# VectorE's two-operand work is moved from between a drive and its recurrence to behind the recurrence

## What is computed

```python
x = x + attention(gn(x))      # layer 0: 12 heads of 32, softmax over 1024 keys, a 5x5 depthwise
                              #          term ("lepe"), a gate o, a projection
x = x + selective_scan(gn(x)) # layer 1: 4 directions, 384 channels, 16 states, 1024 steps
x = x + shift_blur(gn(x))     # layer 2: shift by an offset, then a 5x5 Gaussian, per 8 channels
x = x + attention_se(gn(x))   # layer 3: one head, squeeze-and-excite gate, projection, batch norm

def step(h, inp):             # the recurrence of layer 1
    dtt, ut, bt, ct = inp
    dA = jnp.exp(dtt[..., None] * A)
    h = h * dA + (dtt * ut)[..., None] * bt[:, :, None, :]
    y = jnp.einsum('bkdn,bkn->bkd', h, ct)
    return (h, y)
```

## Time and profile before

| what | value |
| --- | --- |
| median of 3 runs | 10391.47 us |
| profiled execution, its own time | 10405.13 us |
| its span in the profile | 10403.3 us |
| VectorE (DVE) busy | 8089.8 us, 78% |
| TensorE (PE) busy | 7344.5 us, 71% |
| GpSimd (POOL) busy | 4789.0 us, 46% |
| ScalarE (ACT) busy | 4060.0 us, 39% |
| mean granted clock of TensorE | 0.786 |

### The profile page before, as it was taken

How to read it: one execution, slowest core, us unless ns; L and a number is a source line. 1 busy time by engine, 2 the same in 40 slices (tenths; PEclk the granted TensorE clock), 3 DMA queues, 4 the chain that set the end, 5 groups by cost and what they waited for, 6 DMA issues and landing times.

```text
span 10403.3 us, 101295 instructions
## 1 busy us (share of the span) xinstructions
PE 7344.5 (71%) x33720; PEld 3729.0 (36%) x33720; DVE 8089.8 (78%) x5527; ACT 4060.0 (39%) x4186; POOL 4789.0 (46%) x1990
## 2 busy tenths in 40 slices
PE   6757775777758777586776777677775777757556
PEld 2233334433334333342234432343333433244333
DVE  5477888778885888768987688876888678887992
ACT  3333443344433444334443345433443334433431
POOL 2154554345553454435644355434555345543660
PEclk8857877888769878688887878787886888868657
DMA  0174457544574445744566445664447544575782
GB/s 26 42 234 160 164 184 235 197 144 165 187 250 164 159 165 201 237 159 160 174 216 220 158 163 170 234 198 162 164 163 246 196 154 160 189 232 198 253 272 58
DMA packets 717961, 1875.97 MB, mean 180 GB/s; under 512 B 258896, under 2 KB 274640, under 8 KB 717264
## 3 DMA queue, kind: packets, MB, share of 16 engines
q1 hardware_dynamic: 717392, 1869.00, 54.0%
HBM read 1772.03 MB, written 71.04 MB: 177 GB/s over the span
## 4 chain that ended last, share of the span: by engine, by line
PE 40%; DVE 32%; issue 14%; ACT 7%; DMA 4%; DVEq 2%; SPq 1%; ACTq 1%; POOL 0%; POOLq 0%
DVE R L1670 14%; PE ps L751 8%; DVE ps L1660 8%; PE ps L883 7%; PE ps L980 5%; ACT R L1180 4%; DVE nmx L1590 4%; PE ps L1068 3%; PE ps L892 3%; PE ps L863 2%; PE ps L953 2%; PE ps L1051 2%; PE ps L963 1%; PE ps L845 1%; PE ps L1037 1%
## 5 line engine op out<-in xcount | busy, mean ns | idle before, releaser
L1353 POOL TENSOR_TENSOR R<-R 128x1024 f32<-128x1024 f32 x1536 | 3673.5, 2392 | 4302.2 <-DVE ps L1660 4198.6
L1670 DVE TENSOR_TENSOR_SCAN R<-R,ps 128x1024 f32<-128x1024 f32 x1536 | 3508.0, 2284 | 176.3 <-ACT R L1239 62.7
L1239 ACT ACTIVATE R<-R,negA 128x1024 f32<-128x1024 f32 x1536 | 1749.4, 1143 | 2313.4 <-DVE R L1670 2273.6
L980 PE MATMUL ps<-ident,R 128*128 128x128 f32 x12288 | 2146.9, 335 | 587.6 <-POOL R L1353 545.9
L980 PEld LDWEIGHTS ps<-ident,R 128*128 128x128 f32 x12288 | 1806.3, 175 | 1576.1 <-issue 775.2
L1660 DVE TENSOR_TENSOR ps<-R 128x1024 f32<-128x1024 f32 x1536 | 2030.5, 1322 | 162.1 <-DMA R<-bc_scratch 53.7
L1180 ACT ACTIVATE R<-ps 128x1024 f32<-128x1024 f32 x768 | 785.6, 1023 | 1061.8 <-PE ps L883 1061.8
L863 PE MATMUL ps<-R 32*128 32x512 f32 x3072 | 660.1, 943 | 678.8 <-DVE nmx L1590 585.7
L883 PE MATMUL ps<-R 64*128 64x512 f32 x3072 | 900.9, 665 | 203.2 <-ACT R L1180 108.0
L1590 DVE TENSOR_REDUCE nmx<-ps 128x4 f32<-128x2048 f32 x384 | 873.4, 2282 | 193.8 <-PE ps L863 190.6
L751 PE MATMUL ps<-R 128*128 128x512 f32 (+1 forms) x1824 | 879.2, 640 | 201.9 <-DVE R L1525 142.2
(11 more groups left out here) (157 smaller groups left out, 5615.0 us busy)
## 6 DMA issues: line engine op xcount, KB each, us to landing
R<-bc_scratch SPq DMA_DIRECT2D x3072, 512.0 KB, 4.5
R<-in_x SPq DMA_DIRECT2D x72, 512.0 KB, 7.1
out<-R SPq DMA_DIRECT2D x72, 512.0 KB, 5.3
R<-shift_scratch SPq DMA_DIRECT2D x48, 640.0 KB, 7.4
R<-R SPq DMA_DIRECT2D x192, 128.0 KB
R<-out SPq DMA_DIRECT2D x48, 512.0 KB, 8.4
R<-in_w_qkvo SPq DMA_DIRECT2D x32, 576.0 KB, 8.3
rows_scratch<-R SPq DMA_DIRECT2D x24, 512.0 KB, 7.4
```

The source lines that it names most:

```text
L980: mm = pe.matmul(ps[:, 4 + b // 4, (b % 4) * P:(b % 4 + 1) * P], state[i % HELD][:, b * P:(b + 1) * P], ident[:, :], start=fresh and i % G ...
L1239: act.activation(decay[i % len(decay)], dt[:, c, :], ACT.Exp, scale=negA[:, col:col + 1]).then_inc(a_sb.h, 1)
L1353: pool.tensor_tensor(state[i % HELD], state[i % HELD], rows_c[slot], ALU.mult).then_inc(hc_sb.h, 1)
L1670: v.tensor_tensor_scan(h, a, b, 0.0, ALU.mult, ALU.add).then_inc(h_sb.h, 1)
```

## The change

`in_order` gets a second rule. From the moment that a "b" is put out, events of the kinds dv, t, O, rg, x2 and bl are held in a list, and they are put out behind the "s" of that step, in their order. Everything else keeps its place. Since all engines sort by this function, the rule holds for all of them; of the six kinds, five are VectorE's alone, and t is VectorE's and GpSimd's.

```diff
+TWO_IN_SBUF = {("dv",), ("t",), ("O",), ("rg",), ("x2",), ("bl",)}
+
+
 def in_order(*groups):
     out, reader, put_off = [], None, []
+    drive, behind = None, []
     for _, ev in sorted((pe for g in groups for pe in g), key=lambda pe: pe[0]):
+        if ev[0] == "b":
+            drive = ev
+        elif drive is not None and ev[0:1] in TWO_IN_SBUF:
+            behind.append(ev)
+            continue
+        elif ev[0] == "s":
+            out += [ev] + behind
+            drive, behind = None, []
+            continue
         if ev[0] in "xd" and reader is not None:
             put_off.append(ev)
             continue
```

## The result

| kernel | median | runs | ratio to before, 95% interval |
| --- | --- | --- | --- |
| before | 10397.50 us | 4 | |
| after | 10538.41 us | 4 | 1.0132 [1.0117, 1.0146] |

The kernel became slower, by 141 us in the medians and by 131.1 us in the two profiled executions (10536.23 after, 10405.13 before). The prediction said slower, by 60. The sign was right, and so was the mechanism in plain recurrence. The size was less than half of what was measured: two terms, named at the end, were far too small.

The account below looks back on a forecast made before the run. VectorE and the TensorE-ScalarE pair, which share bank 0, take turns as the bound. Losses of 81.1 us less gains of 21.0 make +60 us, 10452 us; forecast's own range 10415 to 10490, 8 in 10 within 10350 to 10505.

Parts of the forecast that it names:

- step 56: Eight t at step 56: the small L1514 waits 2.7 us for T's end, 2.2 us each, 17.6 us lost.
- loop's edge: Seven t at step 190: same mechanism as in plain recurrence, 1.85 us each, 13.0 us lost.
- step 24, the blur load: Seven t at step 24: late z delays SP's C row and the last blur load, 1.0 us each, 7.0 lost.
- The stall of dv costs nothing: Depthwise taps L1609: 175.5 us of waiting goes, gain zero because the wait at O takes it up; bounds 0 and -175.5.
- The gains of O and L1525, 21.0 us: Second O of the second group starts 0.7 us sooner (4.2 us); L1525 at the image's end 2.4 us sooner (16.8).
- t is the part that costs, through z behind T and two late drives: Plain recurrence: GpSimd idles under s, z follows T, two drives take 3.08 us instead of one; +1.85 us per t.
- 21 among the exponentials: t at steps 88, 120, 152, in halves where O waits 5 to 12 us: 0, or +1.85 each without that cover.
- 21 among the row maxima: t at steps 72, 104, 136: R hides T but for 0.6 us each, 12.6 us lost; bounds 0 and 38.9.
- 7 at step 40 beside the second attention: t at step 40: L1720 waits some 2.7 us for T instead of 0.43, 2.3 us each, 16.1 us lost.
- The signs named beforehand: dv at 1.28 us, L1609 near 340; two 3.08 us drives per t; L1514 or L1720 about 2.8; L1525 2.4 sooner.
- Rival C: Row maxima: GpSimd never catches up, blur load fully late, gains at L1525 don't come; +118 us, 10510 us; 10%.
- Rival B: Drives after t: T's lost cover is free, b always gets in first; only the gains count, 10370 us; 13%.

Follow-up runs that it names:

- run 1: The whole change without t (dv, O, rg and x2 behind s), against the kernel before: 0.9973 [0.9962, 0.9984], 10374.05 us.
- run 3: Only dv moved behind s, against the kernel before: 0.9996 [0.9988, 1.0005].
- run 7: Only t of steps 88, 120 and 152 (exponentials) moved behind s, against the kernel before: 1.0005 [0.9996, 1.0013].
- run 6: Only t of steps 72, 104 and 136 (row maxima) moved behind s, against the kernel before: 1.0068 [1.0054, 1.0081], 10484.89 us.
- run 9: Only t of steps 72, 104 and 136 moved, with GpSimd making z before T, against the kernel before: 1.0015 [1.0006, 1.0024].
- run 11: Only t of steps 72, 104 and 136 moved, plus throwaway TensorE matmuls at the maxima, against the kernel before: 1.0033 [1.0021, 1.0046].
- run 10: Only t of steps 72, 104 and 136 moved, SP's four maxima loads one step sooner, against the kernel before: 1.0058 [1.0044, 1.0071], 10462.15 us.
- run 2: Only t moved behind s, at all steps, against the kernel before: 1.0125 [1.0110, 1.0139], 10540.23 us.
- run 8: Only t of step 40 moved, plus five throwaway TensorE matmuls ahead of its wait there, against the kernel before: 0.9993 [0.9984, 1.0001], 10403.23 us.
- run 14: The kernel before with nothing moved, plus throwaway TensorE matmuls at step 40 and the row maxima, against the kernel before: 0.9988 [0.9979, 0.9997].
- run 5: Only t of step 40 moved behind s, against the kernel before: 1.0009 [1.0000, 1.0018], 10421.46 us.

## Where the prediction was right, and where it was wrong

What t costs by place, as the profiled executions have it: the kernel after against run 1, 162.6 us in all, where 81.1 were summed.

| t moved at | predicted, us | kernel after minus run 1, us |
| --- | --- | --- |
| row maxima and exponentials, steps 64 to 180, first seven images | 12.6 | 76.0, of which 52.1 from the first R to M |
| step 40, seven images, steps 39 to 46 | 16.1 | 44.3 (39.4 by step 54) |
| step 56 | 17.6 | 20.8 |
| loop's edge | 13.0 | 12.4 |
| plain recurrence, steps 64 to 180 of the last image | 13.0 | 12.7 |
| step 24, the blur load | 7.0 | -1.0 |

- **The stall of dv costs nothing**: right, shown by run 3 to within 12 us.
- **The gains of O and L1525, 21.0 us**: right in mechanism at both places; the order without t brought 28 us (interval 17 to 40).
- **t is the part that costs, through z behind T and two late drives**: right in plain recurrence to 0.1 us, and at the loop's edge (2.4 to 2.9 us to step 12, where 1.85 was taken; 0.7 of it is also there without t in most images).
- **"21 among the exponentials", 0**: right (run 7).
- **"21 among the row maxima", 12.6 us**: this is the step that failed. I asked whether R would hide T, and R does. I had to ask whether GpSimd works off the product it is behind before something waits for it. It does not: with R and its depthwise products beside it, it carries the debt for up to nine steps. The waits for L863 that I counted on to let it catch up stand ahead of t in two of the three groups. Measured was 56 to 84 us (run 6; 0.0080 of the time within the whole change). My upper bound of 38.9, with 5.6 for the plain steps, held the late drive alone (21 x 1.85): in the kernel after the drives among the maxima take 6.7 us an image more, 2.2 us for each t, 47 us in all, and that alone is past the bound. Run 9 shows that the root is z behind T, and run 11 that TensorE's clock has a part where the maxima are moved alone. SP's loads behind the C row, which run 10 brings back in time, are late in runs 2 and 6, but not in the kernel after. How the price divides between the late drives and the clock stays open.
- **"7 at step 40 beside the second attention"**, 16.1 us: the second step that failed. L1720 waits as it was said, but the term stopped at VectorE. The local price was 6.3 us instead of 2.3, since TensorE ran its next matmuls at a lower clock behind the wait; with TensorE kept busy (runs 8 and 14) moving this t costs nothing more. Moved alone it cost the whole kernel 0 to 19 us (run 5), and in the kernel after its own stretches hold 44.3 us.
- **The sum**: the losses were 162.6 us instead of 81.1, and these two terms are more than the whole difference. The gains came a little larger than summed (31.5 us in the profiled execution of run 1).
- **The signs named beforehand**: two drives of 3.08 us behind a plain t, L1514 at 2.8 us and L1525 2.4 us nearer to O came as said. L1609 near 340 us came nearly (377.8; 351.8 without t). O's idle time did not grow in the kernel after (335.1 to 304.2), because s moved into it.
- **Rival C** (the backlog spreads, 10510) was nearest in its mechanism: "in the row maxima GpSimd never catches up". Its price was too low, and its other half, that the gains at L1525 don't come, was wrong. My range ended at 10505, and 10538 lies outside.
- **Rival B** (lost cover is free) is out by the number of late drives, 38 to 97.

## What to carry to other kernels

A move that lets an engine idle for one step does not cost that step but everything until its backlog is worked off: follow the late product until the first place where the engine has slack, and price the queues of whoever waits on it, the one that issues DMAs too. Put the product that others wait for ahead of the one that nobody waits for. And where a wait of a few microseconds is added ahead of TensorE, price the matmuls behind it at both clock levels. Ask of a reserve of idle time where it stands: a total over the kernel does not say that it lies behind the place that needs it.

## What the runs showed of the hardware

- Behind waits of TensorE of 2.34 and 1.01 us, with eight matmuls between them, the granted clock was 0.80 over 26 us instead of 1.00, and eight matmuls took 6.24 us instead of 3.70. A wait of 2.20 us in the kernel before (ahead of the matmuls at 3195.50) left it at 1.00. How much waiting it takes was not measured.
- The time from M to the first O of a group comes in two lengths in many of these kernels, for the same instructions. In the kernel before, the first group took 64.6 us in two of the six middle images and 68.8 to 69.2 us in the other four; the granted clock over it was 0.98 in the first two and 0.90 or 0.91 in the others. With throwaway matmuls ahead of it (runs 11 and 14) it took 66.1 or 66.2 us in all seven images, at 0.97. So the length goes with the clock, but what sets it off was not tested: of the four long ones, two came in with the same clock ahead of M (0.63) and the same 1.13 to 1.14 us for the first four matmuls as the short ones. That is one reason why single places gain and lose by 4 us from kernel to kernel, and why a difference of under 10 us at one place should not be read as its own.
- Throwaway matmuls in a wait made this kernel faster by 0.12% (0.9988 [0.9979, 0.9997]) although they compute nothing. They are not free: at step 40 of the unchanged order they made the stretch 2.3 or 4.0 us longer (run 14).
